# A state-space block and a mixture of experts on eight cores: one wide B/C/D projection, a convolution split over two engines, smaller output staging, loads moved to another queue

## What is computed

```python
def _L0_attn_ref(x, ...):                      # E = 2048, S = 16
    xp = x @ in_w.T + in_b
    x_main, x_gate = xp[..., :E], xp[..., E:]
    xc = silu(depthwise_conv3(x_main, conv_w) + conv_b)
    dt = softplus(xc @ dt_w.T + dt_b)
    Bt = xc @ B_w.T + B_b;  Ct = xc @ C_w.T + C_b;  Dt = xc @ D_w.T + D_b
    decay = exp(clip(-dt.mean(-1), -10.0, 10.0))
    u = Bt * Dt
    # state = state * d + u_t ;  y_t = (c_t * state).sum(-1)   over the sequence
    y = ys * silu(x_gate)
    return x + (y @ out_w.T + out_b)

def _L0_ffn_ref(x2, ...):                      # 16 experts of 512, top 4; shared of 2048
    combine = router(x2)
    routed = sum_e combine[:, e] * (relu(x2 @ up_w[e].T)**2 @ down_w[e].T)
    return routed + relu(x2 @ shared_up.T)**2 @ shared_down.T

x = x + layernorm(_L0_attn_ref(layernorm(x)))
x = x + layernorm(_L0_ffn_ref(layernorm(x)))
```

## Time and profile before

| | |
|---|---|
| median of 2 runs | 5814.81 us (5796.05 to 5833.56) |
| the profiled execution | 5801.73 us |
| its span on core 0, from the first to the last instruction | 5800.2 us |
| spans of the 8 cores | 5775.0 to 5800.2 us |
| mean granted TensorE clock, core 0 | 0.856 of full speed |
| busy: PE, DVE, ACT, POOL | 71%, 33%, 22%, 10% of the span |

### The profile page before, as it was taken

One profiled execution on the slowest core, in us unless ns is written; L12 is line 12 of the kernel. 1 busy time (PEld: TensorE's weight loads), 2 busy tenths in 40 slices (PEclk: granted clock), 3 DMA queues, 4 the chain that ended last, 5 costly groups with the idle time before them and its releaser, 6 DMA issues.

```text
span 5800.2 us, 52896 instructions; the slowest of 8 cores (5775.0 to 5800.2 us)
## 1 busy us (share of the span) xinstructions
PE 4111.7 (71%) x16746; PEld 1650.9 (28%) x16746; DVE 1909.9 (33%) x3602; ACT 1254.2 (22%) x1937; POOL 580.1 (10%) x518
## 2 busy tenths in 40 slices
PE   4665555556679675986679675986689665986497
PEld 1222222112234222432234222432234222432143
DVE  2224211033432614233422614244422614232523
ACT  0022111102123121312123122322124022322132
POOL 1102000020200202010200202010200202010201
PEclk8777778778789797998899897998889897998698
DMA  5443555442233222432234222432233221432143
GB/s 99 115 116 87 120 117 119 115 112 84 62 116 139 95 82 72 144 124 78 61 117 142 98 80 59 158 125 74 64 117 138 102 75 50 152 136 68 37 149 109
DMA packets 193006, 595.57 MB, mean 103 GB/s; under 512 B 23490, under 2 KB 31938, under 8 KB 192722
## 3 DMA queue, kind: packets, MB, share of 16 engines
q1 hardware_dynamic: 155810, 503.74, 24.9%
q0 software_dynamic: 32832, 88.32, 8.5%
q10 hardware_dynamic: 4096, 0.14, 0.0%
HBM read 583.82 MB, written 79.92 MB: 114 GB/s over the span
## 4 chain that ended last, share of the span: by engine, by line
PE 58%; DMA 14%; DVE 11%; issue 11%; ACT 5%; POOL 1%; DVEq 1%; ACTq 0%; POOLq 0%; SPq 0%
PE pb L295 52%; DMA rw<-up_wt 4%; DMA rdn<-dn_wt 3%; PE pb L616 2%; DMA up_bf<-rw 2%; DMA dn_bf<-rdn 2%; ACT dtb L539 2%; DVE etmp L505 2%; ACT etmp L536 2%; DMA rw<-in_wt 1%; PE pb L397 1%; PE pb L391 1%; PE pb L544 1%; DVE etmp L502 1%; DMA in_bf<-rw 1%
## 5 line engine op out<-in xcount | busy, mean ns | idle before, releaser
L295 PE MATMUL pb<-zs,rdn 128*128 128x512 f16 x5120 | 1188.4, 395 | 338.6 <-DVE aob L937 210.7
L295 PE MATMUL pb<-h,rw 128*128 128x512 f16 x5120 | 1209.0, 397 | 141.0 <-DMA rw<-up_wt 140.9
L899 ACT ACTIVATE etmp<-pb 128x512 f16<-128x512 f32 x640 | 382.1, 597 | 1973.1 <-PE pb L295 1971.2
L295 PEld LDWEIGHTS pb<-zs,rdn 128*128 128x128 f16 x5120 | 514.8, 101 | 1006.4 <-issue 453.1
L295 PEld LDWEIGHTS pb<-h,rw 128*128 128x128 f16 x5120 | 507.4, 101 | 806.4 <-issue 283.8
L295 PE MATMUL pb<-xm,rw 128*128 128x512 f16 x2048 | 537.4, 407 | 176.2 <-ACT xm L513 176.2
L905 DVE TENSOR_TENSOR zs<-etmp,cw_sb 128x512 f16<-128x512 f16 x512 | 217.8, 425 | 858.1 <-ACT etmp L903 858.1
L941 DVE TENSOR_TENSOR aob<-pb,aob 128x512 f16<-128x512 f32 x256 | 177.0, 692 | 850.0 <-PE pb L295 850.0
L616 PE MATMUL pb<-sg,rw 128*128 128x512 f16 x1024 | 278.6, 437 | 110.9 <-DVE zs L629 86.8
L295 PEld LDWEIGHTS pb<-xm,rw 128*128 128x128 f16 x2048 | 196.0, 100 | 490.3 <-issue 311.3
L903 ACT ACTIVATE etmp<-etmp 128x512 f16<-128x512 f16 x512 | 322.1, 629 | 48.0 <-ACT etmp L899 1.1
(11 more groups left out here) (140 smaller groups left out, 3003.4 us busy)
## 6 DMA issues: line engine op xcount, KB each, us to landing
rw<-up_bf SPq DMA_DIRECT2D x280, 512.0 KB, 5.0
rdn<-dn_bf SPq DMA_DIRECT2D x280, 512.0 KB, 4.8
rw<-in_bf SPq DMA_DIRECT2D x112, 512.0 KB, 3.7
rw<-dt_bf SPq DMA_DIRECT2D x112, 512.0 KB, 3.3
rw<-out_bf SPq DMA_DIRECT2D x56, 512.0 KB, 4.3
rw<-up_wt POOLq DMA_DIRECT2D x40, 512.0 KB, 5.3
up_bf<-rw SPq DMA_DIRECT2D x40, 512.0 KB, 2.7
rdn<-dn_wt POOLq DMA_DIRECT2D x40, 512.0 KB, 5.3
```

Source lines behind the costliest of these rows:

```text
L295: e.matmul(oa, lf(), rf(), start=st, stop=sp)),
L899: op("act", lambda e, bank=bank, ea=ea: e.activation(ea, pb[bank][:, :], AF.Relu), reads=[B_pb[bank]], writes=[B_et16[et]])
```

## The change

Four edits in one:

1. The weights of B, C and D are laid side by side, 80 columns per channel block, with B in columns 0 to 15, C in 32 to 47, D in 64 to 79 and zeros between. `bcd_scan` makes one group of 16 matmuls of 128x80 into bank 6; DVE then reads the three results from partitions 0, 64 and 32 of that bank. The constant `bcd_w` and its f16 copy grow from 768 to 1280 columns.
2. `ostage` has 2 slots instead of 4, and each store is issued right behind its addition instead of behind all four.
3. In the convolution POOL makes the second and the third product into a buffer `ptmp16` of 2 slots, both products of a block into the same slot; DVE makes the first product and adds the two.
4. The `rdn` loads of `j > 0` are issued from POOL's queue, with the semaphore of the casts.

```diff
@@ conv
-                op(eng_, lambda e, ...: e.tensor_scalar(
-                    ea, a[:, XMC * k:XMC * k + 512], c_conv_w[:, 3 * k:3 * k + 1], None, ALU.mult),
-                    reads=[ba[k], B_const], writes=[B_et16[et]])
-                op(eng_, lambda e, ...: e.scalar_tensor_tensor(
-                    ea, a[:, XMC * k + 1:XMC * k + 513], c_conv_w[:, 3 * k + 1:3 * k + 2], ea, ALU.mult, ALU.add),
-                    reads=[ba[k], B_const, B_et16[et]], writes=[B_et16[et]])
-                op(eng_, lambda e, ...: e.scalar_tensor_tensor(
-                    ea, a[:, XMC * k + 2:XMC * k + 514], c_conv_w[:, 3 * k + 2:3 * k + 3], ea, ALU.mult, ALU.add),
-                    reads=[ba[k], B_const, B_et16[et]], writes=[B_et16[et]])
+                pa = ptmp16[:, TT * et:TT * (et + 1)]
+                op("pool", lambda e, ...: e.tensor_scalar(
+                    pa, a[:, XMC * k + 1:XMC * k + 513], c_conv_w[:, 3 * k + 1:3 * k + 2], None, ALU.mult),
+                    reads=[ba[k], B_const], writes=[B_pt16[et]])
+                op("dve", lambda e, ...: e.tensor_scalar(
+                    ea, a[:, XMC * k:XMC * k + 512], c_conv_w[:, 3 * k:3 * k + 1], None, ALU.mult),
+                    reads=[ba[k], B_const], writes=[B_et16[et]])
+                op("dve", lambda e, ea=ea, pa=pa: e.tensor_add(ea, ea, pa),
+                   reads=[B_et16[et], B_pt16[et]], writes=[B_et16[et]])
+                op("pool", lambda e, ...: e.tensor_scalar(
+                    pa, a[:, XMC * k + 2:XMC * k + 514], c_conv_w[:, 3 * k + 2:3 * k + 3], None, ALU.mult),
+                    reads=[ba[k], B_const], writes=[B_pt16[et]])
+                op("dve", lambda e, ea=ea, pa=pa: e.tensor_add(ea, ea, pa),
+                   reads=[B_et16[et], B_pt16[et]], writes=[B_et16[et]])
@@ bcd_scan
-            proj(0, 6, u16[:, :], "u16")
-            proj(2, 7, tmp16[:, :], "tmp16")
+            for c in range(NCH_E):
+                parts.append((
+                    (lambda c=c: c_bcd_bf[:, 80 * c:80 * (c + 1)]),
+                    (lambda c=c, j=j: xc_ap(j, c)),
+                    [B_c_bcd, bxm[c]]))
+            mm_group(6, parts, out_sub=pb[6][0:80, :])
+            op("dve", ... u16[:, :], pb[6][0:16, :], c_bcd_b[:, 0:1], None, ALU.add)
+            op("dve", ... tmp16[:, :], pb[6][64:80, :], c_bcd_b[:, 2:3], None, ALU.add)
             op("dve", lambda e: e.tensor_mul(u16[:, :], u16[:, :], tmp16[:, :]),
-            proj(1, 7, ct16[:, :], "ct16")
+            op("dve", ... ct16[:, :], pb[6][32:48, :], c_bcd_b[:, 1:2], None, ALU.add)
@@ ffn_downs, j > 0
-                        op("sp", lambda e, s=slot, oc=oc, g=g: e.dma_start(
+                        op("pool", lambda e, s=slot, oc=oc, g=g: e.dma_start(
                             rdn[:, 2048 * s:2048 * (s + 1)], dn_bf[oc, g]),
-                            ..., dma=True, sem=f"rdn{slot}")
+                            ..., dma=True, sem=f"rdnc{slot}")
@@ ln5_apply_store
-                    os_ = oc % 4
+                    os_ = oc % 2
                     eng_ = "pool" if oc % 2 == 0 else "dve"
                     op(eng_, lambda e, ...: e.tensor_add(
                         ostage[:, TT * os_:TT * (os_ + 1)], etmp[...], x2[...]),
                         reads=[B_etmp[et], B_x2[oc]], writes=[B_ostage[os_]])
-                for oc in range(w0, w0 + 4):
-                    os_ = oc % 4
                     sid = op("pool", lambda e, ...: e.dma_start(outT[...], ostage[...]),
                         reads=[B_ostage[os_]], dma=True, sem="st")
```

More of the change, by code:

```diff
@@ L129, in build_program @@
     dn_wt = nc.dram_tensor("dn_wt", [8, NGRP, 128, 2048], F32, kind="ExternalInput").ap()
-    bcd_w = nc.dram_tensor("bcd_w", [128, 768], F32, kind="ExternalInput").ap()
+    bcd_w = nc.dram_tensor("bcd_w", [128, 1280], F32, kind="ExternalInput").ap()
     gate_wl = nc.dram_tensor("gate_wl", [128, 128], F32, kind="ExternalInput").ap()
@@ L147, in build_program @@
     dn_bf = nc.dram_tensor("dn_bf", [8, NGRP, 128, 2048], FP16, kind="Internal").ap()
-    bcd_bfd = nc.dram_tensor("bcd_bfd", [128, 768], FP16, kind="Internal").ap()
+    bcd_bfd = nc.dram_tensor("bcd_bfd", [128, 1280], FP16, kind="Internal").ap()
     gate_bfd = nc.dram_tensor("gate_bfd", [128, 128], FP16, kind="Internal").ap()
@@ L184, in build_program @@
         c_bcd_b = sb("c_bcd_b", [16, 3])
-        c_bcd_bf = sb("c_bcd_bf", [128, 768], FP16)
+        c_bcd_bf = sb("c_bcd_bf", [128, 1280], FP16)
         c_gate_bf = sb("c_gate_bf", [128, 128], FP16)
@@ L202, in build_program @@
         zs = sb("zs", [128, 16 * TT], FP16)
-        ostage = sb("ostage", [128, 4 * TT])
+        ostage = sb("ostage", [128, 2 * TT])
+        ptmp16 = sb("ptmp16", [128, 2 * TT], FP16)
         u16 = sb("u16", [16, TT])
@@ L255, in build_program @@
         B_zs = [Buf() for _ in range(16)]
-        B_ostage = [Buf() for _ in range(4)]
+        B_ostage = [Buf() for _ in range(2)]
+        B_pt16 = [Buf(), Buf()]
         B_cwrow = [Buf() for _ in range(5)]
@@ L553, in bcd_scan @@
             bxm = B_xm[j % 2]
[L555 to L567, removed]
-            proj(0, 6, u16[:, :], "u16")
-            proj(2, 7, tmp16[:, :], "tmp16")
+            parts = []
+            for c in range(NCH_E):
[4 more added lines that the diff above has]
+            mm_group(6, parts, out_sub=pb[6][0:80, :])
+            op("dve", lambda e: e.tensor_scalar(
+                u16[:, :], pb[6][0:16, :], c_bcd_b[:, 0:1], None, ALU.add),
+                reads=[B_pb[6], B_const], writes=[B_small["u16"]])
+            op("dve", lambda e: e.tensor_scalar(
+                tmp16[:, :], pb[6][64:80, :], c_bcd_b[:, 2:3], None, ALU.add),
+                reads=[B_pb[6], B_const], writes=[B_small["tmp16"]])
             op("dve", lambda e: e.tensor_mul(u16[:, :], u16[:, :], tmp16[:, :]),
                reads=[B_small["u16"], B_small["tmp16"]], writes=[B_small["u16"]])
-            proj(1, 7, ct16[:, :], "ct16")
+            op("dve", lambda e: e.tensor_scalar(
+                ct16[:, :], pb[6][32:48, :], c_bcd_b[:, 1:2], None, ALU.add),
+                reads=[B_pb[6], B_const], writes=[B_small["ct16"]])
             op("dve", lambda e: e.tensor_scalar(rowA[:, :], pb[0][0:1, :], 10.0, -1.0,
@@ L924, in ffn_downs @@
                     else:
-                        op("sp", lambda e, s=slot, oc=oc, g=g: e.dma_start(
+                        op("pool", lambda e, s=slot, oc=oc, g=g: e.dma_start(
                             rdn[:, 2048 * s:2048 * (s + 1)], dn_bf[oc, g]),
-                            reads=[B_scr["dn"][oc][g]], writes=[B_rdn[slot]], dma=True, sem=f"rdn{slot}")
+                            reads=[B_scr["dn"][oc][g]], writes=[B_rdn[slot]], dma=True, sem=f"rdnc{slot}")
                     bank = 6 + (oc % 2)
@@ L1068, in host_layout @@
                    .reshape(8, 5, 128, 2048))
-    bcd = [w.T.reshape(16, 128, 16).transpose(1, 0, 2).reshape(128, 256)
-           for w in (B_w, C_w, D_w)]
-    d["bcd_w"] = f(np.concatenate(bcd, axis=1))
+    bcd = np.zeros((128, 16, 80), np.float32)
+    for i, w in enumerate((B_w, C_w, D_w)):
+        bcd[:, :, 32 * i:32 * i + 16] = w.T.reshape(16, 128, 16).transpose(1, 0, 2)
+    d["bcd_w"] = f(bcd.reshape(128, 1280))
     d["gate_wl"] = f(gate_w.T.reshape(8, 128, 16).transpose(1, 0, 2).reshape(128, 128))
```

15 lines of the change are left out of this document (7 added, 8 removed).

## The result

The change makes the kernel slower by 7.5%: ratio 1.0751 of the changed kernel to the kernel before, 95% interval 1.0687 to 1.0815. Against the 5801.7 us of the profiled execution of before that is about 6237 us. The direction was forecast; the forecast of 6058 us (+4.2% against the median of before, 256 us above the 5801.7) has little more than half of the loss, and the measured time lies above its upper end of 6195.

The account below looks back on a forecast made before the run. PE was taken as bound by unbroken stretches plus chains behind L513 and L629; 5801.7 - 48 (projection) + 122 (staging) + 175 (convolution) + 0 (rdn loads) + 2 (bcd_w) = 6053, shifted to 6058 us; range 5900 to 6195.

Parts of the forecast that it names:

- What bounds the kernel: PE: unbroken 229.5 us stretches per tile; otherwise gaps, chiefly waits behind L513 (176.2 us) and L629 (86.8 us).
- the three signs: Signs of being wrong: convolution chunk stays at 2 us, boundary grows under 10 us, PE waits for rdn in tiles 1 to 7.
- The chain of DVE operations: B, C, D projection: four small DVE operations follow one matmul group; rowB's matmul path is 6.0 us shorter per tile.
- The working: Tile boundary: additions and stores on two slots summed forward from the ready first half to L629, +16 us per boundary.
- P = 0.85: Convolution: assumed us per POOL multiplication, the middle of 0.57 and 1.13, as no row showed it.
- bounds are 1.13 and the 0.35: Convolution: limits in us for one POOL multiplication, from POOL's own two-input operation and DVE's time for the same work.
- the dear case: Rival, convolution: POOL multiplication 1.13 us, chunk 3.62, total 6125 us, or 6211 with slow stores; chance 0.12 for dear or slow.
- do they overlap? Rows say no: Convolution: POOL and DVE exclude each other, so a chunk takes 3.06 us; without exclusion 2.36.
- 2P + 1.36: Convolution chunk: two POOL multiplications plus 1.36 us of DVE work and gaps, 3.06 us against 1.98, +17.3 per tile.
- The estimate from "GPSIMD Engine Reference": Convolution: 769 ns for a best-case 512-element loop would give a chunk of 2.90 us, whole forecast about 20 us lower.
- The first tile: First tile's convolution: POOL weight casts delayed behind the new POOL operations, +54 us instead of 17.
- The rival of late rdn loads: Rdn loads on POOL's queue: landings of 8.0 us would add 121 us, total 6179; chance 0.09.

Follow-up runs that it names:

- e5: Changed kernel, still 2 staging slots, with one store semaphore per slot instead of a coarse one: tile 692.7 us, 13.6 shorter.
- e7: Changed kernel with POOL's convolution products written as f32 instead of f16: multiplications 1.562 us, tile 709.8 us.
- e8: Changed kernel with POOL making 256 columns of each product and DVE the rest: multiplications 0.95 and 0.92 us, tile 689.2 us.
- e9: Changed kernel with a constant for the weight column in both POOL products: 1.49 us for the second product, 1.61 for the first.
- e10: Kernel before the change with all layer-norm multiplications, subtractions and additions on DVE, none on POOL: tile 643.1 us, -12.3.
- e6: Changed kernel with separate buffers for POOL's second and third products, so POOL never waits for DVE's first addition: chunk 3.20 us, tile 689.3 us.
- e4: Kernel before the change with only the rdn loads of tiles 1 to 7 moved to POOL's queue: tile 658.0 us, +2.7.

## Why the prediction was wrong

**What bounds the kernel** was right: the unbroken stretches are the same 229.5 us, and nearly all of the loss is in the chains behind L513 and L629. The sign followed from that. None of the three signs came that the prediction had named for being wrong (a chunk still at 2 us, a boundary longer by under 10, a wait for rdn in tiles 1 to 7): the chains were the right ones, and their lengths were not.

**Edit 1** was forecast at -6.0 us per tile and gave -4.5 alone. The chain of DVE operations came nearly as worked out (rowB's matmul 5.6 us earlier after the start of the projection); what was missed is the clock of that small matmul (1.86 us instead of 1.01 after a longer idle time).

**Edit 2** was forecast at +16 us per boundary and gave +21.8 alone. The mechanism is the one named, a coarse semaphore with two slots, and e5 shows it. The working missed two things. Addition 1 waits as well: its slot was used in the tile before, and the coarse wait takes in store 0 of this tile, issued just ahead (DVE L980 at 3439.85 waited 6.47 us; the working had it in parallel with addition 0). And each store begins some 0.57 us after its addition, where the working had 0.1 for a hand-over. Against these, the second half's operations took 5.4 us on POOL instead of 7.3.

**Edit 3** is where the prediction failed: forecast +17.3 us per tile, measured +32.7 alone. The step is "P = 0.85", with "bounds are 1.13 and the 0.35". P is 1.56 us, outside the bounds, and it has this value in L513 with nothing on DVE beside it. The upper bound assumed that one input can't cost POOL more than two; e7, e8 and e9 show that the time is the operation's own: some 2.5 ns per column, the same whether it writes f16 or f32, with 0.08 us for the column scalar. A row of another operation was taken as a ceiling, and it was none. With P = 1.56 the dear case (3.62) was still too cheap.

The step "do they overlap? Rows say no" failed too, in the other direction. 2P + 1.36 would be 4.48 us with the true P; measured is 4.05, which is 1.56 + 1.69 and 0.8 for DVE's first addition with the waits around it. DVE's second addition and next multiplication run beside POOL's next instruction and cost the chunk no more than the 0.13 us by which L504 is longer than L513. So this error hid a part of the first: with the true P and the step as it stood the chunk would have been forecast too dear. The rows on which the step rested were of two-input operations on both engines, and for these e10 agrees that the pair is slower than DVE alone. The rule of the Trainium skill, "SBUF — State Buffer", section "Who interferes with whom", has a DVE instruction with two inputs in SBUF contend with a POOL instruction that reads SBUF, and calls that contention an exclusive lock, held (the section says so of another DVE mode) for a whole instruction; the prediction had read it as that for these two as well. The traces agree that the two contend, and not that the addition waits for a whole instruction: here an addition of 0.42 us that began 0.12 us after a POOL multiplication of 1.68 us took 0.84 and had ended 0.7 us before POOL's. The estimate from "GPSIMD Engine Reference", section "Elementwise — side-by-side cycle accounting" (769 ns for 512 elements), was low by a factor of two: 1.56 us measured. The sum of the dear case alone is 6123 us, not 6125; nothing hangs on it.

**The first tile** was forecast with its 48 us more (54 for the casts and the chunks, less 6) and came out at some 66: up to the first stretch core 4 has 1770.7 us against 1653.1, 117.6 more, of which 51 belong to tile 1. The mechanism is as forecast: POOL issued five casts together at the end of the convolution, at 348.5 us (forecast 341), and behind them came the chain of one load per 8.8 us, whose last was issued at 479.2 us (forecast 469, before 415.3).

**Edit 4** was forecast at 0 and gave +2.7. The rival of late rdn loads fell: they land in 3.6 us.

The sum of the misses per tile is 15.4 for edit 3, 5.8 for edit 2, 1.5 for edit 1 and 2.7 for edit 4, 25.4 us; over seven tiles 178, and with the first tile's 18 it is 196. Between the forecast's 256 and the 443 of core 4 lie 187. The rest of 9 is of the size of what the four edits together give less than one by one (50.9 against 52.7 per tile, 13 over seven). The range failed because its upper end put the dear POOL case at P = 1.13: a price that no row shows had been bounded by an operation of another form.

## What to carry to other kernels

Moving work to an idle engine pays only if that engine's price for that very form of operation is known: here two multiplications took 3.25 us on POOL and replaced 0.75 + 0.75 us of DVE by additions of 0.42 and 0.83, and the chain that PE waits for got longer. A row of another form on the same engine bounds nothing from above. When a ring of buffers is made smaller, write down for each reuse what its wait covers: with a semaphore that is shared by all stores, every addition but the first waited for the newest store, and a semaphore per slot gave 13.6 of 21.8 us back.

## What the runs showed of the hardware

- POOL's tensor_scalar of 128x512 in f16 takes 1.56 us with nothing on DVE beside it, more than its own tensor_tensor in f32 (1.13); with f32 output it takes the same 1.562, with a constant 1.49, with 256 columns 0.92 to 0.95.
- A two-input f16 addition on DVE that begins 0.12 to 0.19 us after POOL's one-input multiplication takes 0.84 to 0.77 us instead of 0.42 and leaves POOL's at 1.56. A DVE multiplication beside it either takes its 0.34 us and POOL's takes 1.68, or is held to the end of POOL's (0.82 us in e6, 0.56 in e7) and POOL's takes 1.56. F32 operations with two inputs on both engines take 1.6 us a pair, while DVE alone does two in 1.25.
- Weight loads split over two queues (SP and POOL) landed in 3.7 and 4.0 us (core 0 of e4; 3.3 and 3.6 on core 4 of the changed kernel), on one queue in 5.0 and 4.8, with the same bytes per tile and no gain for PE, which had not waited for them.
